# Expert rows sorted in two groups: the last batch routed beside the first group's tiles, early batches finished beside the second's

## What is computed

```python
logits = jnp.einsum('btd,de->bte', x, Wg) + bg
top2_vals, top2_idx = jax.lax.top_k(logits, 2)
scores = jax.nn.softmax(top2_vals, axis=-1)
...
h = jnp.einsum('btd,edh->bteh', x, W1) + b1[None, None]     # E = 8 experts, H = 512
h = jax.nn.gelu(h, approximate=False)
y = jnp.einsum('bteh,ehd->bted', h, W2) + b2[None, None]
out = jnp.einsum('bted,bte->btd', y, combine)
return _layer_norm(x + out, gamma, beta)
```

## Time and profile before

| what | us |
|---|---|
| median of 3 runs (1637.74 to 1648.77) | 1639.59 |
| the profiled execution, its own time | 1636.53 |
| its span, first to last instruction | 1634.8 |
| busy in the span: PE, PE weight loads | 1327.0, 798.3 |
| busy in the span: DVE, ACT, POOL | 934.6, 851.8, 600.4 |
| PE busy in 60 to 1160 us | 948.6 |
| PE busy in 1590 to 1634.8 us | 0.0 |

### The profile page before, as it was taken

How to read it: one execution, slowest core, us unless ns; L and a number is a source line. 1 busy time by engine, 2 the same in 40 slices (tenths; PEclk the granted TensorE clock), 3 DMA queues, 4 the chain that set the end, 5 groups by cost and what they waited for, 6 DMA issues and landing times.

```text
span 1634.8 us, 27815 instructions
## 1 busy us (share of the span) xinstructions
PE 1327.0 (81%) x9189; PEld 798.3 (49%) x9189; DVE 934.6 (57%) x3262; ACT 851.8 (52%) x1642; POOL 600.4 (37%) x768
## 2 busy tenths in 40 slices
PE   3878888988888789889988988988888884599970
PEld 1223444554455445545445444544555553488860
DVE  5355755565756576656555764555554654265655
ACT  3665665656565556555654665444424531255533
POOL 1010322233253335333423442235325444265554
PEclk7878999999999999989998999899979987699985
DMA  7060990000000000000000000001010000212222
GB/s 288 1 229 1 8 3 1 1 7 8 1 14 8 7 1 21 1 7 3 19 1 8 8 8 1 7 8 59 8 43 36 1 11 22 90 54 55 58 90 104
DMA packets 63051, 53.17 MB, mean 33 GB/s; under 512 B 39752, under 2 KB 49488, under 8 KB 62656
## 3 DMA queue, kind: packets, MB, share of 16 engines
q1 hardware_dynamic: 58592, 42.47, 13.2%
q0 software_dynamic: 4320, 8.92, 1.6%
HBM read 20.56 MB, written 30.81 MB: 31 GB/s over the span
## 4 chain that ended last, share of the span: by engine, by line
PE 59%; DVE 17%; ACT 14%; issue 7%; POOL 2%; DMA 1%; POOLq 1%; SPq 0%; DVEq 0%; ACTq 0%
PE scores L1529 10%; PE work L1469 8%; PE outs L1675 7%; PE outs L1548 6%; DVE scores L1085 5%; ACT a_buf L824 5%; PE work L1578 4%; PE scores L1498 3%; DVE ra L1078 3%; PE scores L1662 3%; PE work L1561 3%; ACT ra L830 3%; PE outs L1860 2%; ACT rsum L836 2%; PE work L1559 2%
## 5 line engine op out<-in xcount | busy, mean ns | idle before, releaser
L1085 DVE CUSTOM_DVE_ANT_0 scores<-scores,mask_qk 128x512 f32<-128x512 f32 (+3 forms) x512 | 239.3, 520 | 240.8 <-PE scores L1498 238.1
L824 ACT ACTIVATE a_buf<-scores 128x1024 f32<-128x1024 f32 x256 | 248.0, 1026 | 110.7 <-PE scores L1662 101.4
L676 POOL TENSOR_SCALAR_AFFINE_SELECT big<-big 128x256 f32<-128x256 f32 x256 | 100.9, 407 | 541.5 <-ACT big L818 540.7
L818 ACT ACTIVATE big<-scores 128x1024 f32<-128x1024 f32 (+1 forms) x192 | 169.2, 882 | 231.0 <-PE scores L1529 224.5
L1529 PE MATMUL scores<-ra 64*128 64x512 f32 (+3 forms) x1536 | 188.8, 352 | 47.2 <-ACT a_buf L824 33.0
L686 POOL TENSOR_TENSOR big<-big 128x768 f32<-128x768 f32 x64 | 118.6, 1854 | 191.2 <-PE work L1561 191.0
L1529 PEld LDWEIGHTS scores<-ra 64*128 64x128 f32 x1536 | 124.4, 193 | 109.4 <-ACT a_buf L824 42.3
L1548 PE MATMUL outs<-big 128*64 128x512 f32 (+3 forms) x1024 | 164.8, 449 | 2.2 <-DVE yT L1109 2.2
L1675 PE MATMUL outs<-a_buf 128*16 128x512 f32 x1024 | 148.4, 655 | 8.6 <-DVE wqkv_lo L1032 4.9
L1109 DVE TENSOR_TENSOR yT<-outs,rsum 128x512 f32<-128x512 f32 x64 | 44.3, 692 | 148.4 <-ACT rsum L841 148.4
L1548 PEld LDWEIGHTS outs<-big 128*64 128x64 f32 x1024 | 64.2, 137 | 115.9 <-issue 103.4
(11 more groups left out here) (216 smaller groups left out, 2600.7 us busy)
## 6 DMA issues: line engine op xcount, KB each, us to landing
sorted_rows<-xrows SPq DMA_DIRECT2D x33, 520.0 KB, 6.8
big<-sorted_rows SPq DMA_DIRECT2D x71, 65.0 KB
a_buf<-in_w SPq DMA_DIRECT2D x2, 2048.0 KB, 8.2
a_buf<-choice_rows SPq DMA_DIRECT2D x16, 256.0 KB, 4.9
a_buf<-in_x SPq DMA_DIRECT2D x8, 256.0 KB, 2.9
x_rows<-x SPq DMA_DIRECT2D x8, 256.0 KB, 2.0
ra<-x_rows SPq DMA_DIRECT2D x8, 256.0 KB
out<-a_buf SPq DMA_DIRECT2D x8, 256.0 KB, 2.0
```

The lines of the kernel that those rows point to most:

```text
L818: activation(prob1(g, i), d[:, :, 0:256] if i == 2 else d, ACT.Exp, scale=SCALE1).then_inc(unit_free("pair", g, i), 1)
L824: activation(prob0(c)[:, i * 1024:(i + 1) * 1024], unit_wait(act, "cosine", c, i), ACT.Exp).then_inc(unit_free("cosine", c, i), 1)
L1085: return v.tensor_tensor_reduce(scores_, scores_, mask_qk[:, SEQ - width:SEQ], -1.0, 3e38, ALU.add, ALU.min, neg_max[:, qt, j:j + 1])
```

## The change

The 8 batches become two groups, EARLY (batches 0 to 4, 47 tiles) and LATE (batches 5 to 7, 31 tiles); each has its own regions in `sorted_rows`, its own counts and its own tables. The pass after the last one stops after its step p=0. The tables of EARLY are computed at step (6, 7), and the tile loop starts with EARLY's tiles. Batch 7's routing is placed into the iterations of that loop, behind each engine's own tile work (`AT_PROJ` to `AT_TABLES`): projection at iteration 1, inverse deviation 2, standardizing 4, second rows 6, transposition 7, logits and choice 10, the Exp for the gates (with a load of its table) 12, ranks 16, slots and gates 18, two sends in each of 21 to 24, LATE's tables 27. Since the `work` banks are now needed by that routing, the tile's transposition and output have one bank each, in `outs`.

The reload of x3 stands after tile 46's load, the loads of EARLY's result rows (ten) after tile 54's. Batches 0 to 4 are finished in iterations 53 to 74, one per four iterations: `summed` at 53, inverse deviation 54, `shifted` 55, ACT 56, `scaled` 57, `add_x3` 58, and so on. Batches 5 to 7 are finished at the end as before, in a slightly different order. The tables move out of `big` into a buffer of their own, the constants for them are made at the program's start, and the weight folding moves from step (-2, 0) to step (-2, 6). The zero fill of `sorted_rows` grows from 33 to 34 parts.

```diff
@@ -49,13 +49,46 @@
...
+class Group:
...
+    def __init__(self, first, last, tile, base):
+        self.first, self.last, self.tile, self.base = first, last, tile, base
+        rows = CHOICES * SEQ * (last - first)
+        self.slots = TILES * (last - first)
+        self.size = (rows + EXPERTS * (P - 1)) // P
+        self.end = tile + self.size
+        self.blocks = EXPERTS * self.slots + SPARE
+
+
+EARLY = Group(0, 5, 0, 0)
+LATE = Group(5, BATCH, EARLY.end, EARLY.blocks)
+GROUPS = (EARLY, LATE)
+ALL_TILES = LATE.end
+TABLE = EARLY.size + 1
+BLOCKS = EARLY.blocks + LATE.blocks
...
@@ -89,6 +122,27 @@
...
+def early_steps():
+
+    for o in steps():
+        if o.i < LAST_PASS or o.p == 0:
+            yield o
...
+LAST_T = BATCH - 1
+AT_PROJ, AT_ROWS, AT_SECOND, AT_ROWS_T = 1, 4, 6, 7
+AT_LOGITS, AT_RANK, AT_SLOTS, AT_SEND, AT_TABLES = 10, 16, 18, 21, 27
+FINISH_AT, FINISH_EVERY = LATE.tile + 6, 4
+
+
+def finish_at(n, late):
+
+    k = n - FINISH_AT - late
+    return k // FINISH_EVERY if k >= 0 and k % FINISH_EVERY == 0 and \
+        k // FINISH_EVERY < EARLY.last else None
...
@@ -543,8 +603,7 @@
         def unit_free(*unit):
             return score_free[UNIT_NO[unit] % 2]
 
-        def xt_bank(n):
-            return work[:, n % 2, 0:P]
+        xt_bank, y_bank = outs[:, 1, 0:P], outs[:, 0, 0:DIM]
...
+            def sorted_tiles(first, end):
+
+                for n in range(first, end):
+                    if n >= RING:
+                        sp.wait_ge(y_tile_sent[n % RING], 16 * (n // RING))
+                    at = sp.value_load(block_at[0:1, n:n + 1], min_val=0, max_val=BLOCKS - 1)
+                    sp.dma_start(x_tile(n), sorted_rows[bass.ds(at * P, P), :]).then_inc(
+                        x_tile_in[n % RING], 16)
+
+            def chosen_rows(group):
+
+                for n in range(RING):
+                    sp.wait_ge(y_tile_sent[n], 16 * tiles_in_slot(group.end, n))
+                for b in range(group.first, group.last):
+                    for k in range(CHOICES):
+                        at = k * TOKENS + b * SEQ
+                        sp.dma_start(chosen(b, k), choice_rows[at:at + SEQ, :].rearrange(
+                            "(p t) d -> p t d", p=P)).then_inc(chosen_in[b], 16)
+
+            def finished_rows(group):
+
+                for b in range(group.first, group.last):
+                    sp.wait_ge(out_ready, b + 1)
+                    sp.dma_start(out[b], chosen(b, 0)).then_inc(out_sent, 16)
+
+            sp.wait_ge(rows_sent, 16 * CHOICES * TILES * EARLY.last)
+            sp.wait_ge(tables_ready, 1)
+            sp.wait_ge(out_full[0], ALL_PAIRS)
+            sorted_tiles(0, AT_TABLES)
+            sp.wait_ge(x3_ready, BATCH)
+            sp.dma_start(x3_rows[LAST_T], x3[:]).then_inc(kept, 16)
+            sorted_tiles(AT_TABLES, EARLY.end)
+            sp.wait_ge(kept, 16 * BATCH)
+            for b in range(BATCH):
+                sp.dma_start(x3_kept(b), x3_rows[b]).then_inc(x3_back, 16)
             sp.wait_ge(rows_sent, 16 * CHOICES * TILES * BATCH)
-            sp.wait_ge(tables_ready, 1)
-            for n in range(MAX_TILES):
-                if n >= RING:
-                    sp.wait_ge(y_tile_sent[n % RING], 16 * (n // RING))
-                at = sp.value_load(block_at[0:1, n:n + 1], min_val=0, max_val=BLOCKS - 1)
-                sp.dma_start(x_tile(n), sorted_rows[bass.ds(at * P, P), :]).then_inc(
-                    x_tile_in[n % RING], 16)
-                if n == RING:
-                    sp.wait_ge(kept, 16 * BATCH)
-                    for b in range(BATCH):
-                        sp.dma_start(x3_kept(b), x3_rows[b]).then_inc(x3_back, 16)
-
-            for n in range(RING):
-                sp.wait_ge(y_tile_sent[n], 16 * ((MAX_TILES - n + RING - 1) // RING))
-            sp.wait_ge(y_full, MAX_TILES)
-            for b in range(BATCH):
-                for k in range(CHOICES):
-                    at = k * TOKENS + b * SEQ
-                    sp.dma_start(chosen(b, k), choice_rows[at:at + SEQ, :].rearrange(
-                        "(p t) d -> p t d", p=P)).then_inc(chosen_in[b], 16)
-            for b in range(BATCH):
-                sp.wait_ge(out_ready, b + 1)
-                sp.dma_start(out[b], chosen(b, 0)).then_inc(out_sent, 16)
+            sp.wait_ge(tables_ready, 2)
+            sorted_tiles(EARLY.end, EARLY.end + RING)
+            chosen_rows(EARLY)
+            sorted_tiles(EARLY.end + RING, ALL_TILES)
+            finished_rows(EARLY)
+            sp.wait_ge(y_full, ALL_TILES)
+            chosen_rows(LATE)
+            finished_rows(LATE)
             sp.wait_ge(out_sent, 16 * BATCH)
...
@@ -762,31 +844,43 @@
                                         b2_1_sb[:, bass.ds(chunk * (DIM // CH1), DIM)],
                                         ALU.add).then_inc(xb_ready, 1)
 
+            def add_x3(b):
+
+                pool.wait_ge(rows_ready["fin"], b + 1)
+                nc.gpsimd.tensor_tensor(chosen(b, 0), chosen(b, 0), x3_kept(b),
+                                        ALU.add).then_inc(out_ready, 1)
+
             pool.wait_ge(sparse_in, 16 * N_SPARSE)
             pool.wait_ge(tables_ready, 1)
             biased(0)
             biased(1)
-            for n in range(MAX_TILES):
-                if n + 2 < MAX_TILES:
+            for n in range(ALL_TILES):
+                if n + 2 < ALL_TILES:
+                    if n + 2 == LATE.tile:
+                        pool.wait_ge(tables_ready, 2)
+                        pool.wait_ge(x3_back, 16 * BATCH)
                     biased(n + 2)
                 pool.wait_ge(y_ready, n + 1)
                 nc.gpsimd.indirect_dma_start(
                     choice_rows, bass.IndirectOffsetOnAxis(
                         x_tile(n)[:, ID:ID + 1].bitcast(I32), 0),
                     y_tile(n), None).then_inc(y_tile_sent[n % RING], 16)
-
-            def add_x3(b):
-
-                pool.wait_ge(rows_ready["fin"], b + 1)
-                nc.gpsimd.tensor_tensor(chosen(b, 0), chosen(b, 0), x3_kept(b),
-                                        ALU.add).then_inc(out_ready, 1)
-
-            pool.wait_ge(x3_back, 16 * BATCH)
-            for b in range(BATCH):
+                if n == AT_PROJ + 1:
+                    inverse_deviations("l1", LAST_T)
+                if n == AT_SECOND:
+                    second_rows(LAST_T)
+                if AT_SEND <= n < AT_SEND + TILES:
+                    send_rows(LAST_T, (n - AT_SEND,))
+                if finish_at(n, 5) is not None:
+                    add_x3(finish_at(n, 5))
+                if finish_at(n, 1) is not None:
+                    inverse_deviations("fin", finish_at(n, 1), finish_at(n, 1) % 2)
+
+            for b in range(LATE.first, LATE.last):
                 inverse_deviations("fin", b, b % 2)
-                if b:
+                if b > LATE.first:
                     add_x3(b - 1)
-            add_x3(BATCH - 1)
+            add_x3(LAST_T)
 
         @block.scalar
...
+            def standardized(b):
+
                 act.wait_ge(shift_ready, b + 1)
                 for t in range(TILES):
                     last = activation(chosen(b, 0)[:, t, :], chosen(b, 0)[:, t, :], ACT.Identity,
                                       bias=shift[:, b % 2, t:t + 1], scale=rstd[:, b % 2, t:t + 1])
                 last.then_inc(fin_scaled, 1)
+
+            act.wait_ge(tables_ready, 1)
+            for n in range(3):
+                x_hi_part(n)
+            for n in range(ALL_TILES):
+                if n + 3 < ALL_TILES:
+                    x_hi_part(n + 3)
+                if n == LATE.tile:
+                    act.wait_ge(tables_ready, 2)
+                hidden_gelu(n)
+                if n == AT_ROWS_T:
+                    moved(xnT[:], "xnT", LAST_T)
+                if n == AT_LOGITS + 2:
+                    exp_tables()
+                    second_weight(LAST_T)
+                if finish_at(n, 3) is not None:
+                    standardized(finish_at(n, 3))
+            for b in range(LATE.first, LATE.last):
+                standardized(b)
 
         @block.vector
...
                 v.tensor_tensor(gap[:], top2[:], top1[:], ALU.subtract).then_inc(gap_ready, 1)
-                if t:
+                if t == LATE.first:
+                    v.memset(taken_sum[:, 0, :], 0.0)
+                elif t:
                     v.tensor_copy(taken_sum[:, 0, :], taken_sum[:, TILES, :])
...
-                if (o.i, p) == (-2, 0):
+                if (o.i, p) == (-2, 6):
                     weights_folded()
+                if (o.i, p) == (EARLY.last + 1, 7):
+                    dve.wait_ge(sparse_step, 2)
+                    tables(EARLY)
...
+            for n in range(3):
+                x_lo_part(n)
+            hidden_moved(0)
+            for n in range(ALL_TILES + 1):
+                if n + 3 < ALL_TILES:
+                    x_lo_part(n + 3)
+                if n + 1 < ALL_TILES:
```

(62 more changed lines are left out.)

218 lines of the change are left out of this document (112 added, 106 removed).

## The result

The median after is 1672.02 us over five runs (1653.17 to 1674.14), against 1639.59 for the kernel before in the same series (1624.03 to 1648.77). The ratio is 1.0183, 95% interval 1.012 to 1.0245: slower, and outside the range.

The account below looks back on a forecast made before the run. Three serial pieces were taken to bound the kernel: batch 7's routing, the tiles, the end. -36.2 + 59.3 - 23 + 3.5 = +3.6 us gave 1640.1 against 1636.5, 1643 against the median; own range 1626 to 1656, with rivals 1617 to 1662.

Parts of the forecast that it names:

- The start: Between attention and the tiles: SyncE waits only for the last weighted sum, so the first transposition comes 36.2 us sooner.
- The end: After the last write of results: five batches fewer to finish at 4.46 us each, -23 us with a slightly better order.
- The price of one bank: Tile loop: one PSUM bank instead of two for transposition and for output costs nothing in a quiet tile.
- The two stops by bulk loads: Reloads of kept rows before tile 47 still cost 9.8 us; ten early-batch loads behind tile 54 add 11.3.
- Finishing the early batches: Tiles behind 55: VectorE's insertions and its wait for GpSimd's inverse deviation stop TensorE, +25.1 us (5 to 32).
- The base of 2.13: Tile loop: a tile takes at least 2.13 us, bound by TensorE; the other 0.25 of 2.38 is waits for rows.
- batch 7 beside tiles 0 to 34: Early tiles: TensorE work +5.8 us, VectorE insertions +3.1, ScalarE table loads +1.0, sends with tables +8.5.
- the ring waits: Tile loop: rows come in time where TensorE stops for other reasons; only tiles 31 to 46 keep waits, -10.4 us.
- The end's new order: Finishing the last three batches at the end in a slightly better order saves under 1 us.
- Faster (VectorE hides it): Rival: VectorE's idle time, 47 us over 78 tiles, takes the insertions of about 35; 1618 us, chance 0.25.
- Slower (GpSimd's lateness reaches the ring): Rival: from tile 58 GpSimd's late writes delay loads, and the sends' lateness adds to the tables; 1658 us, chance 0.2.
- The table loads on ScalarE: Exp among Gelu needs two table loads of 1.28 us, without a drain; +1.0 us (0 to 2.6).

Follow-up runs that it names:

- shift later: The changed kernel with the shift and what follows it one tile later, and GpSimd's inverse deviation ahead of its addition: 1661.01 us, ratio 1.0087.
- two banks: The changed kernel with two PSUM banks again for the tiles' transposition and output from tile 22 on: 247.9 us for the tile stage, 3.37 per tile behind 55.
- filler: The changed kernel with 8 useless transpositions per iteration on TensorE from iteration 53 on: 3.83 us per tile instead of 4.22, 76.0 us for tiles 57 to 77.
- beside, in pieces: The changed kernel with two banks from tile 22, loads spread, sends spaced, routing and early finishing cut into pieces: 1619.44 us, ratio 0.9884 to the kernel before.
- the sends apart: The changed kernel with batch 7's eight sends two at a time at tiles 19, 21, 23, 25 instead of 21 to 24: 1669.3 and 1669.0 us.

## Why the prediction was wrong, step by step

**Right.** The start: 39.5 to 3.8 us, -35.7 for -36.2 predicted, first transposition at 1359.93 (1363 was said). The end: -25.1 for -23. The first write to the last took 3.3 us per tile (2.9 to 3 was said). The first tables, +3 predicted, 3 to 5 measured; the folding nothing visible for +0.5, though TensorE's wait for it grew from 4.9 to 8.8 us and was made up, which the prediction did not say. The price of one bank. The two stops by bulk loads are where they were put, a little cheaper: tiles 47 and 48 lose 10.8 - 2 x 2.13 = 6.5 (9.8 predicted), tiles 55 to 57 lose 16.1 - 3 x 2.13 = 9.7 (11.3). Behind tile 55 the shift waits for the inverse deviation five times, 2.4 us once and 3.6 four times (2.5 to 4 was said).

The stage in stretches, the working of the prediction put on each, against the first profile after:

| tiles | as predicted | measured |
|---|---|---|
| 0 to 34 | 89.8 | 100.1 |
| 34 to 46 | 28.6 | 28.4 |
| 46 to 57 | 44.5 | 40.6 |
| 57 to 77 | 67.7 | 85.7 |
| 77 to the last write | 10.3 | 11.2 |

The first is before's 89.7 without its bulk stop (9.8), plus 5.8 + 3.1 + 1.0 + 8.5 and less 34 x 0.25; the second 12 x 2.38; the third 11 x 2.13 + 9.8 + 11.3; the fourth 20 x 2.13 + 25.1; the last is what before took behind its tile 70. Cut this way the prediction's stage is 240.9, 4 us under its sum (185.4 + 59.3).

**The step that failed: "Finishing the early batches", +25.1, with the restarts behind its stalls put at "a tenth of 3.7".** It measured 85.7 - 20 x 2.13 = 43.1, 18 us more. The mechanism was right: the waits come where they were put. The size was wrong, since the term left the clock out. TensorE's idle time in these tiles is 20.6 + 5.8 = 26.4 us, almost the predicted sum. Most of the rest is TensorE busy longer for the same work: 59.6 us of busy time here, 45.1 for 20 tiles of the variant that finishes everything at the end, 14.5 us more. The prediction charged each stall with its idle time alone, and put the restarts, +6 in all, into the range and not into the sum. The tenth had no row behind it; a stall of 6 us cost 3.7 of restart, and the step took it that one of 2 us would cost a tenth of that. The run with useless matmuls shows the term by itself, with VectorE's waits unchanged.

The base of 2.13 was too low as well. With all batches finished at the end the same 20 tiles take 49.1 us, not 42.6. Against that the finishing cost 36.6 us: 22.8 more of idle time (26.4 against 3.6) and the rest in busy time.

TensorE in 20 tiles from tile 57 on, five kernels (the stretches and the groups by form):

| kernel | 20 tiles, us | PE busy | clock | idle in the groups |
|---|---|---|---|---|
| changed | 85.7 | 59.6 | 0.84 | 26.4 |
| shift later | 67.0 | 53.3 | 0.87 | 13.7 |
| two banks | 67.2 | 51.4 | 0.92 | 15.6 |
| filler (21.0 of it useless) | 76.0 | 64.4 | 1.00 | 11.6 |
| beside, in pieces | 54.1 | 47.1 | 1.00 | 6.9 |

Idle and clock go together, though not strictly: each us of stop removed gives back half a us more or somewhat above it in the first rows ((85.7 - 67.0) / (26.4 - 13.7) = 1.5 for the shift, 1.7 for the two banks), but the first profile with the sends apart has 27.8 us of idle time at a clock of 0.90, in 83.0 us.

**A second term, smaller: batch 7 beside tiles 0 to 34, and the ring waits.** 100.1 us for 89.8 predicted in the first profile; 107.8 in the second, with the stop at tile 29. The 2.1 for the routing in it does not follow from the prediction's own price, 3.8 - 1.03 = 2.8. The prediction subtracted the ring waits there (8.5 of the -10.4), since TensorE would stop for other reasons. The periods show both: tile 5 takes 7.4 us (3.9 in before), tiles 15 and 16 take 4.7 and 4.5 (the choice), 31 to 33 take 4.1, 4.9 and 3.9 (the tables), and the tiles between still take up to 3.2. With two banks from tile 22 and the tables in three pieces, 31 to 33 take 8.6 us instead of 12.9; with two banks alone it is 12.0, so it is the pieces that help. What the sends cost was put at 8.5 with the tables; in four of the six profiles with one bank and the sends one tile after the other (the expectation above counts seven), a stop of some 5 us at tile 29 comes to it.

**The end's new order** was put at under 1 us, and it cannot be read from the three batches left: with eight it gives 6.3. The earlier trace rows would have shown it. The shift waits there until the sum of its own batch and then the inverse deviation have passed one after the other, and in the new order the next batch's sum stands beside the inverse deviation. It would have been a gain without any second group.

**The median against the profiled execution.** The prediction shifted its sum by 3.1. The sum for the profiled executions missed by 1653.2 - 1640.1 = 13: 21.3 in the tile stage and 0.5 at its start, less 2.1 at the end and 6.8 before the tiles, where the attention stage happened to end 3.3 us earlier than in before instead of 3.5 later. That is luck, and the medians don't have it: they missed by 29. Of the other 16, the attention stage explains some 9, since it ends some 6 us later on average than in the kernels with one group (twelve profiles against four; the tables explain 3 to 5 of them) and not 3.3 earlier. Some 7 stay open; the stop at tile 29 would fit, but it is not shown that executions without a profile have it.

**The rivals.** Faster (VectorE hides it) falls for this kernel: the insertions stop TensorE, as the argument against it said. The variant in pieces comes out at 1619, near its 1618, but by another sum, so that is a coincidence. Slower (GpSimd's lateness reaches the ring) named the right side, with 1658 for a median of 1672, by the wrong mechanism: behind tile 57 GpSimd waits for VectorE's gate, up to 3.2 us, so it is early, not late. Its other half, that the sends' lateness adds to the tables, is not shown: spacing the sends did not shorten tiles 29 to 33.

**The table loads on ScalarE.** Timeline of ACT in the kernel after, the exponential of batch 7's gates between two tiles:

```profile
1406.85 1.14 ACT L1071 ACTIVATE big<-scores,b_sb 128x128 f32<-128x128 f32 x4 [2.90 <-PE scores L1999]
1408.00 1.28 ACT L902 ACT_TABLE_LOAD   x1
1409.30 0.20 ACT L981 ACTIVATE eg<-gap 128x4 f32<-128x4 f32 x1
1409.41 0.25 ACT L1061 CAST x_hi<-outs 128x128 fp32r<-128x128 f32 x1
1409.67 1.28 ACT L1071 ACT_TABLE_LOAD   x1
1410.97 1.14 ACT L1071 ACTIVATE big<-scores,b_sb 128x128 f32<-128x128 f32 x4
```

A load starts 0.01 us behind the activation before it and the next one 0.02 behind the load, so a switch costs the 1.28 us of the load alone, as the sum had it. The Trainium skill ("ScalarE: Activation LUTs", What ACT_TABLE_LOAD costs) counts a drain of 1.38 us beside it; no such gap is in these rows, and the measurement decides.

**What stays open.** Whether the stop at tile 29 exists without a profile, what the sends alone cost, and how the 10.3 us that tiles 0 to 34 take beyond the prediction divide among the insertions and the ring waits.

## What to carry to other kernels

A stall that is shorter than a tile is not priced by its idle time if it comes again every few tiles: look at the granted clock and at the duration of one matmul before and after such a stop, and charge all the work between two stops at the slower duration. Work that is put beside a tight loop should go in pieces that fit the slack of one iteration, each in an iteration of its own, and no engine of the loop should wait there for another's result of the same iteration. Here a tile then took 2.70 us with the finishing beside it, against 2.46 with none and 4.29 in the changed kernel. Where the loop has no second buffer, give it one over the stretch in which work is inserted (85.7 to 67.2 us for 20 tiles, by that alone). And where stops come in some profiles only, compare how many records the profiles hold before you look for a cause in the kernel.

## What the runs showed of the hardware

- Useless work made a stage faster: 161 matmuls, 21.0 us of TensorE, in 20 tiles took these from 85.7 to 76.0 us, with the granted clock at 1.00 instead of 0.84.
- With stops of 1 to 3 us in most of the tiles the granted clock was 0.84 over 86 us, of which TensorE was busy 59.6: five of 20 transpositions took 0.42 to 0.45 us instead of 0.27. With 6.9 us of idle in 54 it stayed at 1.00.
- Six profiles with 9456 to 9573 semaphore updates show a stop of some 3 to 5 us at tile 27 or 29, six with 10638 to 10703 show none: a profile with missing records can show stops that others of the same code do not.
- The attention stage, with the same instructions, ended up to 30 us apart from one execution to the next, and a change of 6 us (the end's order) can't be seen in medians of up to 19 runs; the stage's own length in one profile shows it.
